# Another order of the instructions in a recurrent loop that runs an LSTM, a delta rule and an RNN side by side

## What is computed

```python
# LSTM (L2_cond), h0 = cond
a = xw_t + prev_h @ Wh
i, f, o = sigmoid(a[:, :H]), sigmoid(a[:, H:2*H]), sigmoid(a[:, 2*H:3*H])
next_c = f * prev_c + i * tanh(a[:, 3*H:])
next_h = o * tanh(next_c)
# delta rule (L2_attn) on the LSTM's output, 8 heads of 32
xp = silu(x @ W_in.T)                     # k, v, q, beta are projections of xp
kn = k / (norm(k) + 1e-06)
delta = v - einsum('bhij,bhj->bhi', S, kn)
S = tanh(beta[..., None] * S + delta[..., None] * kn[..., None, :])
Sq = einsum('bhij,bhj->bhi', S, q)
out = Sq * silu(Sq)                       # then times W_out, added to x
# RNN (L2_cond2) on the new x, h0 = cond
h = tanh(x_t @ Wx + prev_h @ Wh + b)
```

## Time and profile before

| | before |
|---|---|
| median of 3 runs | 3473.64 us |
| profiled execution | 3478.83 us, span 3477.0 |
| busy of the span | PE 2897.3 (83%), PE loads 2164.5 (62%), DVE 1842.8 (53%), ACT 1110.5 (32%), POOL 761.8 (22%) |
| mean granted clock | 0.641 of full speed |

### The profile page before, as it was taken

How to read it: one execution, slowest core, us unless ns; L and a number is a source line. 1 busy time by engine, 2 the same in 40 slices (tenths; PEclk the granted TensorE clock), 3 DMA queues, 4 the chain that set the end, 5 groups by cost and what they waited for, 6 DMA issues and landing times. The chain is left out here.

```text
span 3477.0 us, 94868 instructions
## 1 busy us (share of the span) xinstructions
PE 2897.3 (83%) x35915; PEld 2164.5 (62%) x35915; DVE 1842.8 (53%) x7177; ACT 1110.5 (32%) x4414; POOL 761.8 (22%) x1477
## 2 busy tenths in 40 slices
PE   6899999956888894689899899888547789999998
PEld 3557888844555663456666666665314578888755
DVE  3534444464435433456656656654375854444577
ACT  1233222221222232334444444443223432222222
POOL 1111111102200001344544544545101211111000
PEclk9996555556997795555555555555558955555699
DMA  1000000000000001343343343343000000000000
GB/s 74 2 2 0 0 0 0 0 33 1 2 2 0 1 0 58 66 98 71 66 98 71 66 98 71 65 98 71 37 0 1 2 0 0 0 0 0 0 0 12
DMA packets 106860, 101.37 MB, mean 29 GB/s; under 512 B 95616, under 2 KB 95616, under 8 KB 97536
## 3 DMA queue, kind: packets, MB, share of 16 engines
q1 hardware_dynamic: 106624, 98.13, 12.9%
HBM read 89.68 MB, written 8.39 MB: 28 GB/s over the span
## 5 line engine op out<-in xcount | busy, mean ns | idle before, releaser
L574 POOL TENSOR_TENSOR l2r_beta_s<-l2r_state,l2r_beta_f 128x256 f32<-128x256 f32 x512 | 360.5, 725 | 543.8 <-ACT l2r_state L479 528.5
L695 DVE TENSOR_TENSOR l2r_pre<-l2r_o_ps,l2r_beta_s 128x256 f32<-128x256 f32 x512 | 193.4, 419 | 246.0 <-PE l2r_o_ps L374 245.9
L479 ACT ACTIVATE l2r_state<-l2r_pre 128x256 f32<-128x256 f32 x512 | 190.7, 417 | 260.0 <-DVE l2r_pre L695 260.0
L327 PEld LDWEIGHTS l2r_lstm_ps<-l2r_h_ring,l2r_w_part 128*128 128x128 bf16 x3072 | 103.6, 105 | 222.4 <-DVE l2r_h_low L681 220.9
L362 PE MATMUL l2r_d_ps<-l2r_state,l2r_kq 128*32 128x128 f32 x2056 | 206.8, 421 | 36.4 <-ACT l2r_state L479 36.3
L327 PE MATMUL l2r_lstm_ps<-l2r_h_ring,l2r_w_part 128*128 128x8 bf16 x3072 | 123.4, 169 | 121.7 <-DVE l2r_h_low L681 121.7
L374 PE MATMUL l2r_o_ps<-l2r_rows,l2r_outer 32*128 32x128 f32 x2048 | 207.8, 496 | 15.9 <-DVE l2r_rows L687 15.9
L469 ACT ACTIVATE l2r_lstm_ps<-l2r_lstm_ps 128x24 f32<-128x24 f32 x256 | 44.8, 175 | 392.0 <-PE l2r_lstm_ps L327 391.9
L340 PEld LDWEIGHTS l2r_r_ps<-l2r_r_ring,main_even_layers 128*128 128x128 f32 x512 | 128.8, 311 | 59.3 <-issue 47.1
L340 PE MATMUL l2r_r_ps<-l2r_r_ring,main_even_layers 128*128 128x8 f32 x512 | 149.3, 365 | 9.7 <-ACT l2r_r_ring L487 9.7
L133 PE MATMUL l3r_acc<-l3r_xw,main_base 128*128 x512 | 154.7, 389 | 1.6 <-issue 1.6
(11 more groups left out here) (534 smaller groups left out, 7565.1 us busy)
## 6 DMA issues: line engine op xcount, KB each, us to landing
l2r_beta_f<-l2r_beta_store SPq DMA_DIRECT2D x256, 256.0 KB, 6.1
main_odd_layers<-in_l SPq DMA_DIRECT2D x1, 4826.5 KB, 14.3
l2r_beta_store<-l2r_beta_tok SPq DMA_DIRECT2D x256, 8.0 KB, 1.5
main_odd_layers<-in_l SPq DMA_DIRECT2D x1, 3672.0 KB, 16.0
l2r_v_store<-l2r_v_part SPq DMA_DIRECT2D x128, 24.0 KB, 2.0
l2r_v_rows<-l2r_v_store SPq DMA_DIRECT2D x16, 192.0 KB, 6.3
main_decay<-in_decay SPq DMA_DIRECT2D x1, 3072.0 KB, 11.3
main_even_layers<-in_l SPq DMA_DIRECT2D x1, 2762.5 KB, 9.3
```

Source lines behind the costliest of these rows:

```text
L327: last = nc.tensor.matmul(lstm_ps[:, at + g * B:at + (g + 1) * B], w_part[k][:, g * P:(g + 1) * P], h, start=False, stop=(m == 2), skip_gr ...
L479: nc.scalar.activation(state[:, h * 2 * P:(h + 1) * 2 * P], pre[:, h * 2 * P:(h + 1) * 2 * P], ACT.Tanh).then_inc(state_ready[h], 1)
L574: nc.gpsimd.tensor_tensor(beta_s[:, half], state[:, half], beta_f[:, q % BETA_SLOTS, n % QUARTER, half], ALU.mult).then_inc(s["bs_ready"], 1)
L695: nc.vector.tensor_tensor(pre[:, half].rearrange("p (c n) -> p c n", c=2), o_ps[:, 2 * h:2 * h + 2, 0:P], beta_s[:, half].rearrange("p (c ...
```

## The change

On all engines the order within a step becomes another. On PE the RNN product comes directly behind `retrieve` (in step 0 of a wave behind the outer products), and the LSTM products come behind the outer products; bias and inputs of all four gates stand in front of them in step 0. On ACT `rnn_tanh` comes before `new_state`, the gates behind it. On DVE `lstm_h` and `split_h` of the step before stand behind `masked` and before `summed`; `project` and `output` come behind `summed`. For the first 31 steps (IN_BANK), in which there is no delta rule, h is split in SBUF by two subtractions (`split_alone`), and the products wait for each part by itself. `h_psum` is counted from step 31 on.

```diff
@@ -245,7 +245,7 @@
...
-        h0_rest, h_mid, h_low = mem.sb("h0_rest", [P, B]), mem.sb("h_mid", [P, B], BF16), mem.sb("h_low", [P, B], BF16)
+        h_rest, h_mid, h_low = mem.sb("h_rest", [P, B]), mem.sb("h_mid", [P, B], BF16), mem.sb("h_low", [P, B], BF16)
...
@@ -278,7 +278,7 @@
...
-                 "cell_ready", "tanh_ready", "h_ready", "h_psum", "rest_psum", "mid_h_ready", "low_ready", "xin_psum", "xp_sig_ready", "xp_ready",
+                 "cell_ready", "tanh_ready", "h_ready", "rest_ready", "h_psum", "rest_psum", "mid_h_ready", "low_ready", "xin_psum", "xp_sig_ready", "xp_ready",
...
@@ -300,6 +300,8 @@
...
+        IN_BANK = 2 * TC - 1
...
@@ -320,12 +322,17 @@
 
                 def lstm_products(n):
                     at = n % TC * 4 * B
-                    pe.wait_ge(s["low_ready"], n + 1)
-                    for m, h in enumerate((high(h_ring[:, (n - 1) % SLOTS, :]), h_mid[:, :], h_low[:, :])):
+                    alone = n <= IN_BANK
+                    if not alone:
+                        pe.wait_ge(s["low_ready"], n + 1)
+                    h_parts = high(h_ring[:, (n - 1) % SLOTS, :]), high(h_rest[:, :]) if alone else h_mid[:, :], h_low[:, :]
+                    for m in range(3):
+                        if alone:
+                            pe.wait_ge(s[("h_ready", "rest_ready", "low_ready")[m]], n + 1)
                         for g in range(4):
                             for k in range(3 - m):
-                                last = nc.tensor.matmul(lstm_ps[:, at + g * B:at + (g + 1) * B], w_part[k][:, g * P:(g + 1) * P], h,
-                                                        start=False, stop=(m == 2), skip_group_check=True)
+                                last = nc.tensor.matmul(lstm_ps[:, at + g * B:at + (g + 1) * B], w_part[k][:, g * P:(g + 1) * P],
+                                                        h_parts[m], start=False, stop=(m == 2), skip_group_check=True)
                     last.then_inc(s["gates_psum"], 1)
 
                 def rnn_inputs(w):
@@ -439,21 +446,19 @@
                             values(0)
                         if delta is not None or final:
                             retrieve(n)
-                        if lstm is not None and lstm >= 1 and step == 0:
-                            lstm_bias(lstm)
-                            lstm_inputs(lstm, 0)
-                        elif lstm is not None:
-                            lstm_products(lstm * TC + step)
+                        if rnn is not None and step >= 1:
+                            rnn_product(rnn * TC + step)
                         if delta is not None:
                             spread_delta(n)
-                        if lstm is not None and lstm >= 1 and step == 0:
-                            for g in range(1, 4):
-                                lstm_inputs(lstm, g)
-                            lstm_products(lstm * TC)
-                        if rnn is not None:
-                            if step == 0:
-                                rnn_inputs(rnn)
-                            rnn_product(rnn * TC + step)
+                        if rnn is not None and step == 0:
+                            rnn_inputs(rnn)
+                            rnn_product(rnn * TC)
+                        if lstm is not None:
+                            if lstm >= 1 and step == 0:
+                                lstm_bias(lstm)
+                                for g in range(4):
+                                    lstm_inputs(lstm, g)
+                            lstm_products(lstm * TC + step)
                         if proj is not None:
                             project(proj, step)
                         if out is not None:
@@ -553,14 +558,13 @@
                             project(proj, step)
                         if out is not None:
                             output(out, step)
-                        if lstm is not None:
-                            lstm_gates(lstm * TC + step)
+                        if rnn is not None:
+                            rnn_tanh(rnn * TC + step)
                         if delta is not None:
                             new_state(delta * TC + step)
                         if lstm is not None:
+                            lstm_gates(lstm * TC + step)
                             lstm_tanh(lstm * TC + step)
-                        if rnn is not None:
-                            rnn_tanh(rnn * TC + step)
 
             @block.gpsimd
             def _(pool):
@@ -660,24 +664,32 @@
 
                 def lstm_h(n):
                     at = n % TC * 4 * B
-                    out_gate = lstm_ps[:, at + 2 * B:at + 3 * B]
                     dve.wait_ge(s["tanh_ready"], n + 1)
                     if n % TC == 0 and n >= SLOTS:
                         dve.wait_ge(s["xin_psum"], n // TC - 1)
-                    nc.vector.tensor_tensor(h_ring[:, n % SLOTS, :], out_gate, tanh_c[:, :], ALU.mult).then_inc(s["h_ready"], 1)
-                    nc.vector.tensor_tensor(lstm_ps[:, at + 3 * B:at + 4 * B], out_gate, tanh_c[:, :],
-                                            ALU.mult).then_inc(s["h_psum"], 1)
+                    nc.vector.tensor_tensor(h_ring[:, n % SLOTS, :], lstm_ps[:, at + 2 * B:at + 3 * B], tanh_c[:, :],
+                                            ALU.mult).then_inc(s["h_ready"], 1)
+
+                def split_alone(n):
+                    h = h_ring[:, n % SLOTS, :]
+                    dve.wait_ge(s["h_ready"], n + 2)
+                    nc.vector.tensor_tensor(h_rest[:, :], h, high(h), ALU.subtract).then_inc(s["rest_ready"], 1)
+                    dve.wait_ge(s["rest_ready"], n + 2)
+                    nc.vector.tensor_tensor(h_low[:, :], h_rest[:, :], high(h_rest[:, :]), ALU.subtract).then_inc(s["low_ready"], 1)
 
                 def split_h(n):
                     at = n % TC * 4 * B
+                    count = n - IN_BANK + 1
                     rest = lstm_ps[:, at:at + B]
+                    nc.vector.tensor_tensor(lstm_ps[:, at + 3 * B:at + 4 * B], lstm_ps[:, at + 2 * B:at + 3 * B], tanh_c[:, :],
+                                            ALU.mult).then_inc(s["h_psum"], 1)
                     dve.wait_ge(s["h_ready"], n + 2)
-                    dve.wait_ge(s["h_psum"], n + 1)
+                    dve.wait_ge(s["h_psum"], count)
                     nc.vector.tensor_tensor(rest, lstm_ps[:, at + 3 * B:at + 4 * B], high(h_ring[:, n % SLOTS, :]),
                                             ALU.subtract).then_inc(s["rest_psum"], 1)
-                    dve.wait_ge(s["rest_psum"], n + 1)
+                    dve.wait_ge(s["rest_psum"], count)
                     nc.vector.tensor_copy(h_mid[:, :], high(rest)).then_inc(s["mid_h_ready"], 1)
-                    dve.wait_ge(s["mid_h_ready"], n + 2)
+                    dve.wait_ge(s["mid_h_ready"], count)
                     nc.vector.tensor_tensor(h_low[:, :], rest, h_mid[:, :], ALU.subtract).then_inc(s["low_ready"], 1)
 
                 def masked(n):
@@ -770,31 +782,32 @@
                 nc.vector.tensor_tensor(bias_part[:, 2, :], bias_rest[:, :], high(bias_rest[:, :]),
                                         ALU.subtract).then_inc(s["bias_split"], 1)
                 nc.vector.tensor_copy(selv_bf[:, :], sel_v).then_inc(s["consts_ready"], 1)
-                dve.wait_ge(s["h_ready"], 1)
-                nc.vector.tensor_tensor(h0_rest[:, :], h0, high(h0), ALU.subtract).then_inc(s["mid_h_ready"], 1)
-                dve.wait_ge(s["mid_h_ready"], 1)
-                nc.vector.tensor_copy(h_mid[:, :], high(h0_rest[:, :]))
-                nc.vector.tensor_tensor(h_low[:, :], h0_rest[:, :], high(h0_rest[:, :]), ALU.subtract).then_inc(s["low_ready"], 1)
+                split_alone(-1)
                 for k in range(BODIES + 1):
                     lstm, proj, delta, out, rnn = waves(k)
                     for step in range(TC):
                         final = k == NTC + 2 and step == 0
                         n = (k - 2) * TC + step
+                        if rnn is not None and step == 0:
+                            add_out(rnn)
                         if delta is not None or final:
                             masked(n)
-                        if rnn is not None and step == 0:
-                            add_out(rnn)
+                        before = k * TC + step - 1
+                        if IN_BANK <= before < T:
+                            lstm_h(before)
+                        if IN_BANK <= before < T - 1:
+                            split_h(before)
+                        if delta is not None:
+                            summed(n)
                         if proj is not None:
                             project(proj, step)
                         if out is not None:
                             output(out, step)
-                        if delta is not None:
-                            summed(n)
                         if lstm is not None:
```

(8 more changed lines are left out.)

## The result

The changed kernel takes 3452.02 us (median of 7 runs, 3446.52 to 3465.97), the kernel before in the same runs 3473.64 (7 runs, 3466.23 to 3478.13): ratio 0.9943, 95% interval 0.9924 to 0.9962. It is faster by 21.6 us, where 76 had been forecast; 3452 lies above the range of 3382 to 3438. The profiled execution's span is 3453.4 against 3477.0.

The account below looks back on a forecast made before the run. The prediction took a chain, not a full engine, as the bound: delta rule and LSTM loops tied together, 3.93 us a step. Terms −16, −48, −13 and +1 made −76, from 3473.6 to 3397 us, range 3382 to 3438.

Parts of the forecast that it names:

- The lone steps: LSTM steps of waves 0 and 1 before any delta rule: products no longer wait for the low part, −16 us.
- The plain step: Delta step without extra work: mask to mask 3.25 us, RNN product hidden by the mask at no cost.
- the rivals about that product: RNN product partly covered, 0.1 to 0.2 a step (0.14); wholly in front, 3508 (0.05); or late enough to eat the gain (0.02).
- the LSTM loop: Rival: this loop binds, its slack of 0.10 lost to signalling; 3407 to 3417, up to 3425; chance 0.07.
- the clock: Rival: PE's clock rises above 1.2 GHz because its work is packed closer, about 3300; chance 0.04.
- steps 2 and 12: Steps where PE also waits for DVE's project and output, moved behind the sum: 4.30 and 4.62 us.
- step 0: First step of a wave: bias and input products now all stand behind the outer products, 6.70 us.
- the waves without LSTM: Two waves already at 3.25 a step: lose two waits, gain PE extras, +1 us.
- The sum of a full wave: All sixteen steps of a wave with everything: 61.6 against 65.6 us, −48 over twelve waves.
- step 6: Step with ACT's square root: table, root and table back hold RNN tanh and state, 4.16 us.
- step 7: DVE's chain to the keys, with its reduction behind it, exceeds the gap between sum and cell: 3.55 us.
- The first two delta waves: Waves with delta rule and LSTM, first without RNN and output: 118.0 for 130.8 us, −13.

Follow-up runs that it names:

- the lone part: Kernel before, with only h split in SBUF and LSTM products waiting part by part in the first 31 steps: 3456.88 us, ratio 0.9945 to before.
- the last kernel: Changed kernel plus sigmoid behind step 6's root, xp and transpose before the sum, v stores from ACT, RNN's step-0 work before outer products: 3365.02 us, ratio 0.9691 to before.

## Why the prediction was wrong

**Right.** The lone steps: −16 forecast, −15.0 in the profile, −16.6 in the runs of that part alone. PE's wait for `v_rows` at the start near 13: 12.81. The plain step, 3.25, with the RNN product in front of the outer products at no cost; so the rivals about that product, the LSTM loop and the clock (0.50 to 0.51 in every window) all fell. Steps with projections 3.77 and 3.77, with output products 3.69 and 3.67, steps 2 and 12 of 4.30 and 4.62 against 4.26 and 4.58, step 0 6.70 and 6.78. The first mask, forecast near 1408, came at 1399.30, but the stage as a whole began 10.2 earlier than in the profile before.

**The step that failed** is the last sentence on the costs: "No DMA is moved in SP's queue, only closer together; the waves without LSTM took theirs at 3.25 a step." True of the DMAs, and beside the point: the chain of 41 issues has a length of its own, about 31, from the keys to the landing of `v_rows`, and it is the waves that moved closer together. So the term that the sum had at nothing, PE's wait for `v_rows` at the end of a wave, is 2.33 in a full wave on average. The rows for it were at hand: the earlier trace rows show this very chain with PE waiting 6.26 at its end, and it was read as a matter of the start alone. Full waves had 2.6 to spare on average. From the keys to PE's need lay 33.2 before (1717.98 to 1751.16); with a last step of 3.69, as forecast, it would be 28.5 now (1692.09 to 1717.70 + 3.69 − 0.80), 4.7 less. The chain itself kept its length: 30.6 before and 30.8 after, from the keys to the landing, on average of the twelve waves. 30.8 − 28.5 is 2.3 of wait, and step 15 is 2.33 longer than forecast; in the wave shown it is 31.5 − 28.5, and the row says 2.94. The evidence that the sentence calls on was a single wave, for the last one loads no `v_rows`, and it stood on the edge. Its SP timeline before:

```profile
2368.25 3.63 SPq L832 DMA_DIRECT2D l2r_kn_store<-l2r_kn_tok  x8
...
2390.12 0.36 SPq L861 DMA_DIRECT2D l2r_v_rows<-l2r_v_store  x1
```

and PE's:

```profile
2396.60 0.30 PE L349 MATMUL l2r_d_ps<-l2r_v_rows,l2r_selv_bf 128*32 128x128 bf16 x4
```

There the chain took 21.9 to the issue, not 24.2, and with 6.4 to landing it was done 0.1 before PE wanted it. In the profile of the lone part, where these steps have the order of before, the same chain took 29.7 to the landing, PE waited, and the step lasted 4.90 in place of 3.45: so even at the old length of a step without LSTM the transfer wasn't safe.

**The sum of a full wave**, 61.6 forecast and 65.4 measured: step 15 +2.33 (mean 6.02), step 6 +1.12, step 7 +0.49, step 0 +0.08, step 11 −0.15, the others −0.05. For twelve waves: −48 forecast, −2.7 measured. The first two delta waves: −13 forecast, −3.6 measured, since their ends stand at 9.11 and 4.90, 7.1 of the 9.2 missed; their steps 6, with three loads too (5.04 and 5.12), have most of the rest. The waves without LSTM: +1 forecast, +5.9 measured, of which 3.0 are their one step 15 with a wait for `v_rows` (6.46 for 3.45); the rest is mostly step 12, 4.58 for 3.45 in both waves.

**Step 6** was mis-sized by what isn't in the earlier trace rows: there the gates were the first function behind the root, so one load brought a table that served all. The change put tanh first. That the number of loads depends on which function comes first had no term.

**Step 7** was mis-sized by a duration: `kn_tok` at 0.42 came from a place without POOL's work beside it. At its new place POOL's two products run at the same time, and the first of them starts ahead of it:

```profile
1691.05 1.59 POOL L578 TENSOR_TENSOR l2r_beta_s<-l2r_state,l2r_beta_f 128x256 f32<-128x256 f32 x2 [2.48 <-ACT l2r_state L484]
...
1691.14 0.92 DVE L729 TENSOR_TENSOR l2r_kn_tok<-l2r_k_tok,l2r_inv 128x256 f32<-128x256 f32 x1
```

1.59 for the pair in place of 1.41, so each side costs the other time. No experiment moved POOL's work alone, but the traces are close to one. In each of the eight profiles with the new order the first wave's `kn_tok`, with POOL idle, takes 0.42, and the other fifteen, beside POOL's products, 0.92. The small operation behind the root shows what kind of delay it is. Before:

```profile
1716.61 0.61 POOL L595 TENSOR_TENSOR l2r_v_part<-l2r_v_rest 128x256 bf16<-128x256 f32 x1
...
1716.70 0.56 DVE L710 TENSOR_SCALAR l2r_norm<-l2r_norm 128x8 f32<-128x8 f32 x1
```

It ends 0.03 behind POOL's operation. So it does in all 28 cases in which it starts under that operation, in the profiles of before and of the lone part, also in the one in which it starts 0.38 into it and lasts only 0.26. It is a wait for the other engine's instruction, not a slower pace. It goes the other way too: at step 11 of the new order POOL's product starts under the cell product, takes 0.92 in place of 0.72, and the cell product isn't longer.
The Trainium skill (GPSIMD Engine Reference, Specifications) says that GpSimd shares its SBUF interfaces with VectorE and contends with instructions that have two SBUF inputs or run in a 2-port mode; `kn_tok` and the cell product have two such inputs, and the trace agrees, with 0.92 against 0.42 and 1.16 against 0.68.

**What stays open.** Inside the stage the profiles show −15.5 (lone steps −15.0, masks −0.5); the medians show −21.6, with an interval of 13 to 26. In the single profile of before the stage begins at 1328.35, in the nine of changed kernels between 1314.6 and 1323.6. Nothing ahead of the stage was edited, and the stage's very first instruction is already 5 to 14 us earlier in them. Over the nine changed kernels the medians' gain is between 6.7 us more and 1.9 less than the gain inside the stage. Scatter of that size is on record without any edit: the kernel before ranges from 3466 to 3485 in its seventeen runs, and the mean granted clock is 0.643 to 0.645 in the six shortest and 0.640 to 0.641 in the four longest. That it is the whole of the difference isn't shown.

## What to carry to other kernels

When a loop is to become shorter, list for each queue the chain that it must get through in one round, from the last event that starts it to the first that needs its end, and compare that length with the new round, not with the old; a wait that shows only once, at the start, may be such a chain at 2.6 us from the edge, and here its landing varied by 4 us from wave to wave. Gains that lie within such a chain's stretch are given back by the wait; gains ahead of it stay. Where an activation moves, ask which function is now the first behind a table's change, and if it is a function of several tables, call the one wanted first.

## What the hardware showed unexpectedly

- A one-column sigmoid (0.20 us) behind a root spares a whole table load of 1.28 us: three loads become two, 11 us of the kernel.
- DVE's durations depend on POOL: the product over 128x256 elements takes 0.42 or 0.92 us, the one over 128x512 0.68 or 1.16, and even an operation over eight columns 0.16 or 0.56; wherever this last starts under the POOL operation shown above, it ends 0.03 us behind it, whether that takes 0.26 or 0.58.
- Eight store issues cost SP 3.9 us of its queue in the wave shown (4.6 on average) and ACT nothing that a step shows (0.87 for two), although ACT works in every step.
- PE is busy 98% of the long stretch of the last kernel (705 of 721, modelled ends) at a granted clock of 0.50.
